# A long convolution inside a mixture kernel: from eight block diagonals per head to one block and 128 carried states

## The reference, cut to what matters

```python
# L0_cond: a causal convolution over the 1024 positions, one filter per head
dtA = A * dt[:, None]                                # (head, 64 complex modes)
Cs = Cc * (jnp.exp(dtA) - 1.0) / A
K = 2.0 * einsum('hn,hnl->hl', Cs, exp(dtA[:, :, None] * arange(1024))).real
y = irfft(rfft(u * mask) * rfft(K))[..., :1024] + u * mask * D[:, None]
y = y * mask                                         # mask: position < length[b]
# L0_ffn: a router over 64 experts of rank 16, on every row (b, head) of 1024 numbers
scores = y @ Wr.T;  gates = softmax(top-16 of scores), 0 for the other 48
h = einsum('nd,krd->nkr', y, A)                      # 1024 -> 64 * 16
out = x + 2 * einsum('nkr,kdr->nd', h * gates, B)    # 1024 -> 1024
```

## Time and profile before

| | |
|---|---|
| median of 3 runs | 1048.53 us (1047.22 to 1048.88) |
| the profiled execution | span 1045.5 us, from its first to its last instruction; 14883 instructions |
| TensorE matmul / weight load busy | 987.6 us (94%) / 906.2 us (87%) |
| VectorE, ScalarE, GpSimd busy | 497.7 us (48%), 270.9 us (26%), 33.7 us (3%) |
| DMA | 93.18 MB, mean 89 GB/s |

### The profile page before, as it was taken

One profiled execution on the slowest core, in us unless ns is written; L12 is line 12 of the kernel. 1 busy time (PEld: TensorE's weight loads), 2 busy tenths in 40 slices (PEclk: granted clock), 3 DMA queues, 4 the chain that ended last, 5 costly groups with the idle time before them and its releaser, 6 DMA issues.

```text
span 1045.5 us, 14883 instructions
## 1 busy us (share of the span) xinstructions
PE 987.6 (94%) x5568; PEld 906.2 (87%) x5568; DVE 497.7 (48%) x1216; ACT 270.9 (26%) x418; POOL 33.7 (3%) x22
## 2 busy tenths in 40 slices
PE   0399999999999999999999999999999999999995
PEld 0389988999989999999999999999999999999984
DVE  8894554665553344344434434443443344344321
ACT  4451333333342212122221212222121222212200
POOL 5430000000000000000000000000000000000000
PEclk9999999999999999999999999999999999999998
DMA  4551222212222222222232222222222222222101
GB/s 161 170 201 65 69 90 94 95 64 91 74 91 94 99 93 76 75 76 89 94 99 93 77 76 87 77 93 98 94 81 73 85 78 93 98 95 85 49 33 41
DMA packets 28187, 93.18 MB, mean 89 GB/s; under 512 B 5394, under 2 KB 5522, under 8 KB 28178
## 3 DMA queue, kind: packets, MB, share of 16 engines
q1 hardware_dynamic: 28178, 93.07, 26.6%
HBM read 75.99 MB, written 17.07 MB: 89 GB/s over the span
## 4 chain that ended last, share of the span: by engine, by line
PE 93%; DVE 4%; DMA 1%; ACT 1%; issue 0%; DVEq 0%
PE out_ps L713 23%; PE h_ps L713 16%; PE out_ps L718 11%; PE h_ps L718 8%; PE turn_ps L713 7%; PE conv_ps L705 7%; PE conv_ps L699 6%; PE conv_ps L700 5%; PE turn_ps L718 3%; PE turn_ps L754 3%; PE out_ps L690 2%; DMA out<-wide 1%; PE turn_ps L681 1%; DVE k_work L447 0%; DVE k_work L459 0%; DVE tmp L429 0%
## 5 line engine op out<-in xcount | busy, mean ns | idle before, releaser
L713 PE MATMUL out_ps<-b_hi,g_hi 128*128 128x512 f32 x512 | 203.8, 398 | 0.0
L713 PE MATMUL out_ps<-b_lo,g_hi 128*128 128x512 f32 x512 | 201.1, 393 | 0.0
L713 PE MATMUL h_ps<-a_hi,y_hi 128*128 128x384 f32 x512 | 171.2, 334 | 0.0
L713 PE MATMUL h_ps<-a_lo,y_hi 128*128 128x384 f32 x512 | 171.1, 334 | 0.0
L662 DVE SCALAR_TENSOR_TENSOR wide<-out_ps,gate_scale,x_in 128x512 f32<-128x512 f32 x64 | 48.0, 750 | 214.3 <-PE out_ps L718 214.3
L718 PE MATMUL out_ps<-b_hi,g_lo 128*128 128x512 f32 x512 | 127.7, 392 | 0.0
L718 PEld LDWEIGHTS out_ps<-b_hi,g_lo 128*128 128x128 f32 x512 | 96.2, 188 | 21.0
L713 PEld LDWEIGHTS out_ps<-b_hi,g_hi 128*128 128x128 f32 x512 | 96.8, 189 | 20.0 <-ACT g_hi L390 0.2
L713 PEld LDWEIGHTS out_ps<-b_lo,g_hi 128*128 128x128 f32 x512 | 96.7, 189 | 20.1
L699 PE MATMUL conv_ps<-xt_parts,t_hi 128*128 128x512 f32 (+4 forms) x320 | 114.0, 360 | 0.0
L636 DVE TENSOR_TENSOR wide<-turn_ps,gates 128x256 f32<-128x256 f32 x32 | 13.6, 425 | 204.7 <-DMA out<-wide 204.7
(11 more groups left out here) (133 smaller groups left out, 1148.4 us busy)
## 6 DMA issues: line engine op xcount, KB each, us to landing
t_lo<-k_padded SPq DMA_DIRECT2D x64, 512.0 KB, 9.5
xt_in<-in_xt SPq DMA_DIRECT2D x32, 512.0 KB, 23.7
x_in<-in_x SPq DMA_DIRECT2D x32, 512.0 KB
out<-wide SPq DMA_DIRECT2D x31, 512.0 KB
a_in<-in_a_t SPq DMA_DIRECT2D x8, 512.0 KB, 7.9
b_in<-in_b_t SPq DMA_DIRECT2D x8, 512.0 KB, 6.7
out<-wide SPq DMA_DIRECT2D x2, 256.0 KB
a_in<-in_wr_t SPq DMA_DIRECT2D x1, 256.0 KB, 4.1
```

The lines of the kernel that those rows point to most:

```text
L713: pe.matmul(o, hi[:, c, :], moving[:, c, columns], start=first and c == order[0] and moving is w_hi, stop=False)
```

## The change: what it does, and the diff

The filter is a sum of 64 damped complex modes. Only the block inside a chunk (`d = 0`, 128 x 128 for each head) stays a Toeplitz matrix. What earlier chunks contribute is carried by 128 real states for each head (64 modes, real and imaginary, in the partitions as 16 of one and 16 of the other by turns):

- `feed` (PE): 3 matmuls of 448 columns for each head take each of the first 7 chunks to its own addition to the states, into `conv_ps`.
- `states` (VectorE): the recurrence from chunk to chunk: for each of 6 moves two `scalar_tensor_tensor` on 64 columns (own part, one for each head), one shuffle that exchanges real and imaginary partitions, and two more `scalar_tensor_tensor`. `high_z` and `low_z` split the states.
- `near` (PE): 3 matmuls of 512 columns for each head; `from_states`: 3 of 448, added to the same bank.
- The tables of powers (130 long) are now made for each tile, three tiles ahead: `arguments` and `make_powers` (VectorE), `waves` (ScalarE: one Sin, two Exp), `out_factors`, `low_out`, `low_in`, two transposes (`turn_in`) and two matmuls that sum the filter's row (`kernel_row`, into `k_ps`, now in `h_ps`), `copy_k`, `add_skip`. The row goes to DRAM and comes back as a 128 x 128 block for both heads (128 KB in 512-byte pieces).
- The strips, `conv_far`, `add_far`, the filter building in steps 1 to 7 and their buffers go. `hg` has its own buffer; the output is written in place over `x_in`, so the next x is loaded only after the output has landed (`s_out`).
- The order on SP is now: x transposed, row of the filter, wait, block, output, wait, x in rows. The parameters come in 8 DMAs; steps 29, 30 and 31 are written out.

```diff
-            def load_toeplitz(t, i):
-                sp.dma_start(t_lo[:, i, :].bitcast(F32), toeplitz(t, i)).then_inc(s_t[i], 16)
+            def kernel_rows(t):
+                sp.wait_ge(s_kdone, t + 1)
+                dst = bass.AP(k_dram, t * (HT * KROW) + PAD, [[HT * KROW, 1], [KROW, HT], [1, P]])
+                sp.dma_start(dst, k_sb[:, :, :]).then_inc(s_k, 16)
+            def load_near(t, first=False):
...
+                sp.wait_ge(s_k, 16 * t + 16)
+                sp.sem_inc(s_freed, 1)
+                src = bass.AP(k_dram, t * (HT * KROW), [[1, P], [KROW, HT], [1, P]])
+                sp.dma_start(t_lo[:, :, :].bitcast(F32), src).then_inc(s_t, 16)
...
+            def step(t, prep=True, table=True, last=False):
+                if table:
+                    sp.wait_ge(s_xlo, t + 3)
+                    load_x(t + 3)
+                if prep:
+                    kernel_rows(t + 2)
+                    load_near(t + 2)
...
                     sp.wait_ge(s_o, 2 * t + 2)
-                    sp.dma_start(rows(out, t), o_sb[:, :]).then_inc(s_out, 16)
+                    sp.dma_start(rows(out, t), x_in[:, :]).then_inc(s_out, 16)
+                    sp.wait_ge(s_out, 16 * t + 16)
                     sp.dma_start(x_in[:, :], rows(x, t + 1)).then_inc(s_x, 16)
...
+            def waves(t):
+                act.wait_ge(s_args, t + 1)
+                act.activation(turned[:, :, :, :], args[:, :, :, :], ACT.Sin, scale=TWO_PI).then_inc(s_wave, 1)
+                for i in range(HT):
+                    act.activation(decay[:, i, :], grid[:, 0, :], ACT.Exp, scale=rates[:, bass.ds(HT * t + i, 1)]).then_inc(s_wave, 1)
...
+            # ScalarE, end of a step
+                if prep:
+                    high_x(t + 2)
+                    copy_k(t + 2)
+                if table:
+                    waves(t + 3)
...
+            def states(t):
+                n, moves = HT * t, FED - 1
+                for i in range(HT):
+                    dve.wait_ge(s_fed, n + i + 1)
+                    dve.tensor_copy(z[:, 0, i, :], conv_ps[i][:, 0:B]).then_inc(s_first, 1)
+                dve.wait_ge(s_first, n + HT)
+                for c in range(1, FED):
+                    for i in range(HT):
+                        if c > 1 and i == 0:
+                            dve.wait_ge(s_state, moves * n + HT * (c - 1))
+                        dve.scalar_tensor_tensor(out=part[:, i, :], in0=z[:, c - 1, i, :], scalar=step_own[:, bass.ds(n + i, 1)],
+                                                 in1=conv_ps[i][:, c * B:(c + 1) * B], op0=ALU.mult, op1=ALU.add).then_inc(s_part, 1)
+                    dve.stream_shuffle(swapped[:, :, :], z[:, c - 1, :, :], SWAP).then_inc(s_swap, 1)
+                    dve.wait_ge(s_part, moves * n + HT * c)
+                    for i in range(HT):
+                        if i == 0:
+                            dve.wait_ge(s_swap, moves * t + c)
+                        dve.scalar_tensor_tensor(out=z[:, c, i, :], in0=swapped[:, i, :], scalar=step_other[:, bass.ds(n + i, 1)],
+                                                 in1=part[:, i, :], op0=ALU.mult, op1=ALU.add).then_inc(s_state, 1)
...
+            # VectorE, one step: states(t + 1), router, then
+                if conv:
+                    low_near(t + 1)
+                    low_z(t + 1)
...
+                    if n == 2:
+                        dve.tensor_scalar(gate_sum[:, 1:2], gate_sum[:, 0:1], 1.0 / SCALING, None, ALU.mult).then_inc(s_router, 1)
+                        if prep:
+                            out_factors(t + 2)
...
+            # g_lo, mask_y(t + 1), low_out, low_in (t + 2), low_y(t + 1), low_x(t + 2), arguments(t + 3), reciprocal, output halves
+                    if half == 0:
+                        if prep:
+                            add_skip(t + 2)
+                        if table:
+                            make_powers(t + 3)
...
+                pe.wait_ge(s_hg, 3 * t + 2)
+                turn_hg((7, 6, 5, 4)).then_inc(s_turn, 1)
+                if conv:
+                    near(t + 1)
+                pe.wait_ge(s_hg, 3 * t + 3)
+                turn_hg((3, 2, 1, 0)).then_inc(s_turn, 1)
+                if conv:
+                    from_states(t + 1)
+                if prep:
+                    turn_in(t + 2)
...
                 down_low(0)
+                if prep:
+                    kernel_row(t + 2)
                 down_high(1, (0, 1, 2, 3))
                 down_low(1)
-                if chunk:
-                    build_k(*chunk_build(t))
+                if prep:
+                    feed(t + 2)
```

More of the change, by code:

```diff
@@ new lines, in _ @@
+            split_weights(3)
+            act.wait_ge(s_far, 1)
+            act.activation(far_sin[:, :, :], far_turn[:, :, :], ACT.Sin, scale=TWO_PI).then_inc(s_farwave, 1)
+            act.activation(far_decay[:, :], rates[:, :], ACT.Exp, scale=float(P)).then_inc(s_farwave, 1)
+            high_out(0, first=True)
+            split_weights(4)
+            copy_k(0, first=True)
+            split_weights(5)
+            waves(1)
+            split_weights(6)
+            high_z(0)
+            high_near(0)
@@ new lines, in _, with step @@
+            split_weights(7)
+            split_weights(8)
+            for i in range(HT):
+                high_y(0, i)
+            high_out(1)
+            high_in(1)
+            high_x(1)
+            copy_k(1)
+            waves(2)
+            for i in range(FIRST_B, len(loads) - 3):
+                split_weights(i)
+            def step(t, conv=True, prep=True, table=True, first=False):
+                if conv:
+                    high_near(t + 1)
+                    high_z(t + 1)
@@ L667, in _ @@
             step(0, first=True)
-            with dve.Fori(1, CHUNKS) as t:
-                step(t, chunk=True)
-            with dve.Fori(CHUNKS, TILES - 1) as t:
+            with dve.Fori(LOOP, END) as t:
                 step(t)
-            step(TILES - 1, ahead=False)
+            step(TILES - 3, table=False)
+            step(TILES - 2, prep=False, table=False)
+            step(TILES - 1, conv=False, prep=False, table=False)
         @block.tensor
         def _(pe):
-            def build_k(n, first, heads, buffers):
-                wave = buffers[2]
-                pe.wait_ge(s_factors, n + 1)
-                for h in range(heads):
-                    last = pe.matmul(k_ps[:, h * GRID:(h + 1) * GRID], wave[:, 1, h, :], wave[:, 0, h, :], start=True, stop=True)
-                last.then_inc(s_kps, 1)
@@ L702, in conv_low, with turn_in @@
[L702 to L707 removed]
+            def turn_in(t):
+                pe.wait_ge(s_powers, t + 1)
+                for i in range(HT):
+                    last = pe.transpose(in_ps[:, i, :], powers[:, i, 0, 0:P], ident[:, :])
+                last.then_inc(s_turned, 1)
@@ new lines, in near @@
+            def near(t):
+                pe.wait_ge(s_tlo, t + 1)
+                pe.wait_ge(s_part, HT * (FED - 1) * (t + 1))
+                for i in range(HT):
+                    pe.matmul(conv_ps[i][:, :], t_hi[:, i, :], xt_hi[:, i, :], start=True, stop=False)
+                    pe.matmul(conv_ps[i][:, :], t_hi[:, i, :], xt_lo[:, i, :], start=False, stop=False)
+                    last = pe.matmul(conv_ps[i][:, :], t_lo[:, i, :], xt_hi[:, i, :], start=False, stop=False)
+                last.then_inc(s_near, 1)
```

607 lines of the change are left out of this document (279 added, 328 removed).

## The result

Before: 1048.24 us, after: 1051.41 us (15 runs each); ratio 1.0032, 95% interval [1.0024, 1.004]. The change costs 3 us, 0.3%, which is small but clear of the noise. I had forecast 1017 us, faster than before.

A forecast was written before the change was run, and what follows sets the result against it. It took a VectorE-TensorE-ScalarE loop of 29.3 us a step to bound the kernel. 98.2 to step 1, 820 for steps 1 to 28, 55.2 and 40.3 gave 1014, plus 3.0: 1017 us, range 984 to 1058.

The forecast's parts named there:

- TensorE's floor: TensorE's own work in one loop step without stalls: 28.2 us, 2.2 below the kernel before.
- A move of the recurrence: One of six chunk-to-chunk moves on VectorE, priced at 1.25 us, bounds 0.95 and 1.6.
- S: Length of the whole recurrence on VectorE ahead of the router: six moves and two copies, 7.95 us.
- a cheap recurrence: Rival: a move under 1.07 us lets the loop fall to TensorE's 28.2, total 986 us; chance 0.25.
- VectorE without overlap: Rival: a move's small operations run one after another, 1.5 us a move, step 30.85, total 1060 us; chance 0.19.
- The loop S + 21.35: Recurrence, router, hg, transposes, down, kernel row, tables, powers, second output half set the step: 29.3 us; chance 0.47.
- The output circle: First output half, filter row store, block, output, x in rows again: 27.9 us a turn, hidden under 29.3, barely.
- The third rival: The output circle binds at its upper end, 30.4 us a step, total 1048 us, no change; chance 0.09.
- Set-up: Start up to the first up matmul: 54.8 plus 5 for parameter DMAs, dependent operations and a recurrence, 60 us.
- step 0: First step: 28.2 us of TensorE work plus 10 of stall for low parts, recurrence and a third table.
- what would break the sum: TensorE's clock falling in stalls from 1.00 toward its 1.2 GHz level, making all the forecast times too low.
- End: Step 31, waiting for the last circle: output, x in rows, two halves and two stores, 40.3 us.

The follow-up runs named there:

- e12: e11 with the product of powers and the out factors on VectorE moved behind the third hg; 979.88 us, ratio 0.9348 to the kernel before.
- e1: Changed kernel with x in rows and output each moved as one DMA per head (outermost dimension 64, not 2); 1024.46 us, ratio 0.9774 to the kernel before.
- e7: e1 with another order of weight splits, low parts and near in set-up and step 0 alone; 1016.62 us, ratio 0.9701 to the kernel before.
- e9: Changed kernel with only the load of x in rows split into one transfer per head; 1029.95 us, ratio 0.9831 to the kernel before.
- e10: Changed kernel with only the output store split into one transfer per head; 1023.72 us, ratio 0.9767 to the kernel before.
- e5: e1 with the product of powers moved from between the output halves to behind the next step's second gates product; 1017.02 us, ratio 0.9703 to the kernel before.
- e6: e1 with the last three of six recurrence moves replaced by a copy, leaving out computation; 988.01 us, ratio 0.9426 to the kernel before.
- e11: e5 and e7 together, with feed ahead of the second down half and the recurrence between the output halves; 1011.4 us, ratio 0.9651 to the kernel before.
- e4: Changed kernel with the output back in the buffer of hg and x in rows loaded right behind it; 1170.27 us, ratio 1.1188 to the kernel before.
- e2: Changed kernel with x in rows for step 0 loaded after the last weights; 1054.13 us, ratio 1.0054 to the kernel before.

## Why the prediction was wrong, point by point

- **TensorE's floor, 28.2: right.** 28.39 busy in a step of the changed kernel, 28.06 where nothing waits (e12).
- **A move of the recurrence 1.25, S = 7.95: right** (1.24 to 1.34, 7.93). The rivals of a cheap recurrence (below 1.07) and of VectorE without overlap (1.5) are both out. The sum is nearer than its terms, and that is in part luck. Each own or other part takes 0.28, not 0.22, and the second of a pair starts 0.19 after the first (0.47 for two), not 0.14; against that the pattern took 0.01 for 0.07, and from the second move on the other parts start 0.04 behind the end of the shuffle (0.30, for 0.28) where I had 0.16 of waits. As the two of a pair still overlap, of the two halves of the Trainium skill's sentence ("VectorE: DVE Perf Modes", section on the DRAIN you can't avoid) these rows bear out the second.
- **The loop S + 21.35 = 29.3: right as a sum, but it does not set the step of this kernel.** e1, e7, e9 and e10 all show 29.3, with 0.90 of idle TensorE where I had 1.1. What I missed is a second loop of almost the same length over the second down half (e5: 29.09).
- **The output circle: the step that failed in the loop.** I wrote that it hides under 29.3, "barely", at 27.9. It took 29.5 to 30.3 a turn in the turns read, mean step 29.75. Term by term: output 12.84 (13.0 forecast), x in rows 12.95 and 13.43 (11.8), small store 1.69 (1.4), and some 0.4 more in issues and waits between them: 27.9 - 0.2 + 1.2 to 1.6 + 0.3 + 0.4 = 29.6 to 30.0. The mis-sized term is x in rows. I had priced it from its bytes at 53 GB/s, though the same bytes as output had 13.0 in the earlier trace rows; the upper end of my own bounds, 13.0, was nearly right. The third rival, at 0.09, is what happened. e1, e9 and e10 show it: shorten either transfer and 29.3 appears. The Trainium skill ("DMA: Bandwidth & Descriptors", section on why a DMA increments its semaphore by 16) names what e1 changed, the slowest dimension: 2 before, 64 after, and the transfers went from 13 us to 3 to 4, with a DMA share of 0.84 and 0.90 where the earlier trace rows has 0.13. The 0.45 a step over 28 steps is some 12.5 us.
- **Set-up: 60 forecast, 69.06 measured, and step 0: 38.2 forecast, 47.8 measured. The start is the other step that failed, and the larger.** Together 18.6 late. I had added 5 us up to the first up matmul for a set-up that holds a whole recurrence, which took 10.0 there (38.29 to 48.3 on VectorE); e6, with half of the moves, takes 3.6 off it, and e7's order 2.9. What the rest of these 9 us is was not run. In step 0 I had counted the recurrence and the low parts but not their order: ScalarE's last splits wait behind `high_z`, and the router behind them (e7: 5 us). The stall ahead of the transposes was 15.9 us where I had 10. The low clock that came with it, granted 0.50 and 0.70 in 95 to 100 and 100 to 105, was written down as what would break the sum. Next to step 1, whose clock was 1.00, TensorE's work in step 0 took about 3.4 us more (estimate from the starts: 1.4 in the up stage, 2.0 behind the transposes).
- **End: 40.3 forecast, 42.3 measured**, the same x in rows and store once more.

The misses are 18.6 + 12.5 + 1.9 (step 29) + 0.5 (step 30) + 2.0 = 35.5 us of span, of the 35.7 from 1014 to 1049.7. Had only one of the first two happened, the kernel would have been faster than before (1048.24): without the circle, with steps of 29.3, some 1039 us, and with the forecast's start 1033, both worked out and not run. The 3.0 us that I added for what lies around the span were too many too: a profiled execution's time is 1.8 over its own span (1051.48 against 1049.7; in e1 1024.5 against 1022.7). My only case for slower was a slow recurrence; that two smaller misses of one sign could add up to it had no chance of its own in the forecast.

Why TensorE's own work takes 28.33 in e6 and 28.06 in e12 with the same matmuls can be read in part: 0.23 of the 0.27 lies in near and the second transposes. In e6 the third `hg` still stands behind the out factors and ends at 576.61; the transposes that need it start at 576.66, 0.39 behind the last near matmul, where e12 has 0.23. So 28.33 was not a floor, and e12's order removed a wait in it that the rows of e6 don't list as idle time. The last 0.04 is open.

## What to carry to other kernels

When a change lets a buffer be shared, write down the circle of transfers that it closes, and price each by the longest transfer of the same shape in the trace, not by its bytes; a circle as near to the loop as 27.9 to 29.3 is not safely hidden, and 0.09 was too low a chance for it. Price the start as carefully as the loop: here it missed by more. Count first how many DMA engines a transfer uses: here an edit of one address pattern was worth 2.6% in the changed kernel (1024.46 against 1051.41), and the redesign of the convolution 1.3% where both kernels have it. And look for the second longest loop before removing the longest: e5 gained a quarter of what I expected and e11 nothing, until e12 moved the last term of the next loop.

## What the runs showed of the hardware that I had not expected

- The length of a stall alone did not say whether TensorE's clock falls. In e4 TensorE idles 2.9 to 3.2 us ahead of the transposes in every step of the loop. Around the stalls of 2.85, 3.11 and 3.13 us in steps 1, 3 and 5 the granted clock stayed at 1.00; in steps 2, 4 and 6 it was 0.50, its 1.2 GHz level, for some 3 us, and in the six later steps read for almost 6, from before the stall ended. In e2 stalls of 1.85 and 2.01 us came with 0.50 for some 3 us, and stalls of 1.89 and 1.90 with 1.00. The changed kernel's stalls in the loop, up to 1.89 us, left the transposes at 0.66 us; the granted clock was 1.00 around the four read.
- A VectorE operation that begins just behind a subtraction on GpSimd can take as long as the rest of it. In the changed kernel's set-up a 64-wide operation takes 2.24 us where its like takes 0.22, and ends with GpSimd's:
```profile
20.71 2.35 POOL L278 TENSOR_TENSOR a_lo<-a_in,a_hi 128x1024 fp32r<-128x1024 f32 x1 [5.19 <-ACT a_hi L285]
```
```profile
20.90 2.24 DVE L571 TENSOR_TENSOR tmp<-tmp,er 128x64 f32<-128x64 f32 x1
```
A low part of a 1024-wide weight takes 1.23 us (e2, at 90.11); two of them beside GpSimd's subtractions took 5.93 (73.19 to 79.1), and `z_lo` took 3.23 beside them and 1.08 without. Seven such operations, some 2 us each, stand on VectorE's way to the first up matmul (at 20.90, 26.67, 31.77, 36.07, 40.77, 50.82 and 53.97); the kernel before has at least as many, so they don't explain the miss. A set-up without GpSimd's subtractions was not run.
- The Sin and Exp tables each load in 1.28 us and the activation behind starts at once (e1: 583.78 + 1.28, then 585.07).
